# Spaced gathers, a ring of 28 blocks, a table for the drain, and one product, difference and sum for a tile's query rotations

## The reference, cut to what matters

```python
c_kv = x @ W_dkv                                   # 32 latents per key
I = index scores of 4 heads, local window = +inf, future = -inf
_, idx = top_k(I, 96)                              # 64 local keys and 32 chosen ones per query
key_c, value = (c_kv @ W_uk)[idx], (c_kv @ W_uv)[idx]
query_r = _pope((c_q @ W_qr), angles_q)            # softplus, then a rotation by the position
key_r = _pope((x @ W_kr)[idx], angles_k)           # angle by the rank in the list
scores = (query_c . key_c + query_r . key_r) * scale
out = softmax(scores) @ value                      # 8 heads, then @ W_out
# x1 = LN(x + out); a router picks 1 of 32 experts (capacity 80); x2 = LN(x1 + expert(x1))
# layer 2: 9 shifted gates and values, LN, 8 small experts and a shared one, LN
```

## Time and profile before

| what | value |
|---|---|
| three runs | 1228.55, 1239.28, 1255.21 us, median 1239.28 |
| the profiled execution | 1243.05 us |
| its span | 1240.8 us |
| mean granted TensorE clock | 0.817 of full |
| PE, DVE, ACT, POOL busy | 73%, 56%, 41%, 35% |
| chain that ended last | PE 50%, "another core or an unknown queue" 19%, issue 9%, ACT 9%, DVE 8% |

### The profile page before, as it was taken

One profiled execution on the slowest core, in us unless ns is written; L12 is line 12 of the kernel. 1 busy time (PEld: TensorE's weight loads), 2 busy tenths in 40 slices (PEclk: granted clock), 3 DMA queues, 4 the chain that ended last, 5 costly groups with the idle time before them and its releaser, 6 DMA issues.

```text
span 1240.8 us, 17636 instructions
## 1 busy us (share of the span) xinstructions
PE 909.5 (73%) x5786; PEld 518.2 (42%) x5786; DVE 689.6 (56%) x2059; ACT 509.4 (41%) x1463; POOL 431.8 (35%) x462
## 2 busy tenths in 40 slices
PE   7569639379379878787884965935529998878885
PEld 3235415236136544444442533623316584334443
DVE  4588608248248856573763762936303223887763
ACT  5256405134126646554543551814217322424420
POOL 3400360721710366665636054072640004320120
PEclk9588858679669988886977785966759989988987
DMA  8100211101100011111101010010106151000000
GB/s 227 29 1 22 36 27 26 39 20 33 30 17 4 16 27 22 26 23 22 26 12 26 6 21 19 5 25 14 22 20 175 34 148 44 6 1 10 1 9 17
DMA packets 59641, 39.97 MB, mean 32 GB/s; under 512 B 27072, under 2 KB 51360, under 8 KB 59424
## 3 DMA queue, kind: packets, MB, share of 16 engines
q1 hardware_dynamic: 44064, 23.40, 7.6%
q0 software_dynamic: 12800, 14.15, 5.6%
q10 hardware_dynamic: 2688, 1.31, 0.4%
HBM read 33.31 MB, written 5.55 MB: 31 GB/s over the span
## 4 chain that ended last, share of the span: by engine, by line
PE 50%; another core or an unknown queue 19%; issue 9%; ACT 9%; DVE 8%; DMA 2%; POOL 1%; SPq 0%; ACTq 0%; POOLq 0%; DVEq 0%
PE psK L726 6%; PE psI L636 5%; PE psK L622 4%; PE psP L788 3%; PE psS L762 3%; PE psP L795 3%; PE psS L1731 3%; ACT R L886 2%; PE psP L622 2%; PE psK L714 2%; PE psP L777 2%; PE psS L765 2%; ACT ot_region L1023 1%; PE psS L805 1%
## 5 line engine op out<-in xcount | busy, mean ns | idle before, releaser
L602 POOL DMA_INDIRECT G<-key_rows,idx x320 | 308.9, 965 | 483.3 <-DVEq L1126 238.3
L1014 ACT ACTIVATE PT<-psP 128x256 f32<-128x256 f32 x128 | 49.0, 383 | 408.8 <-remote 292.9
L1295 DVE CUSTOM_DVE_ANT_0 S<-psS,cst 128x208 f32<-128x208 f32 x128 | 47.5, 371 | 270.8 <-remote 207.7
L636 PE MATMUL psI<-kiT,qiT 64*128 64x512 f32 (+5 forms) x320 | 105.4, 675 | 64.9 <-ACT R L886 54.6
L622 PE MATMUL psK<-cst 128*128 128x512 bf16 x335 | 101.1, 416 | 14.5 <-issue 9.3
L762 PE MATMUL psS<-KT,Q 96*32 96x128 f32 x1024 | 70.7, 306 | 43.1 <-issue 26.7
L1099 DVE SCALAR_TENSOR_TENSOR SC<-R,w_i,SC 128x512 f32<-128x512 f32 (+5 forms) x120 | 78.5, 654 | 15.7 <-ACT R L886 12.8
L622 PE MATMUL psP<-cst 128*128 128x512 bf16 x114 | 46.0, 429 | 53.8 <-ACT ot_region L1023 46.9
L886 ACT ACTIVATE R<-psI 128x512 f32<-128x512 f32 (+5 forms) x160 | 73.6, 511 | 15.7 <-remote 6.5
L1129 DVE MAX8 top<-SC 128x8 f32<-128x128 f32 (+15 forms) x64 | 78.5, 1226 | 2.3
L1131 DVE FIND_INDEX8 idxf<-top,SC 128x8 uint32<-128x128 f32 (+15 forms) x64 | 78.3, 1223 | 0.0
(11 more groups left out here) (341 smaller groups left out, 1803.0 us busy)
## 6 DMA issues: line engine op xcount, KB each, us to landing
G<-key_rows,idx POOLq DMA_INDIRECT x320
rtmp<-idx_rows SPq DMA_DIRECT2D x32, 128.0 KB
xslots<-zrow SPq DMA_DIRECT2D x4, 320.0 KB, 9.0
SC<-xslots SPq DMA_DIRECT2D x8, 160.0 KB
yslots<-SC ACTq DMA_DIRECT2D x8, 160.0 KB, 2.9
V<-val_rows SPq DMA_DIRECT2D x15, 80.0 KB
xr<-in_x SPq DMA_DIRECT2D x1, 1024.0 KB, 9.4
qiT<-in_w_gate SPq DMA_DIRECT2D x4, 256.0 KB, 4.2
```

What stands on the lines that cost most here:

```text
L602: pool.indirect_dma_start(ring[o % RING][:, g % GPB, DR:], None, key_rows, bass.IndirectOffsetOnAxis(ap=idx[:, t, g:g + 1], axis=0),).then ...
L636: pe.matmul(psI[i][:, 0:w], lhs, kiT[64 * i:64 * i + 64, CH * c:CH * c + w], start=True, stop=True).then_inc(s["i_mm"], 1)
```

## The change

Five things. (1) **Gathers**: the wait of the second gather for the landing of the block before is gone. Ahead of the second, third and fourth gather of a block GpSimd sets 64 columns of a spare tile to zero and waits for its own increment. (2) **Ring**: four more slots lie in the memory of four weights that are dead after the start, so it has 28 blocks. (3) **Drain**: the stages of each tile have their steps in a table, one step earlier for the last two tiles (two for some), `WARM_T` is 0 and the filler matmuls of the drain have a table too; `place` is cut in two. (4) **Queries**: a tile's four products are one instruction, its differences one and its sums one. (5) **Second part**: the loads of slots go out ahead of those of weights, and a batch's first gather no longer waits for the landing of the batch before. Some semaphores are used twice.

```diff
-RING_G, RING_X = 21, 3
-RING = RING_G + RING_X
+RING_G, RING_X, RING_W = 21, 3, 4
+RING = RING_G + RING_X + RING_W
+SPACE = 64
-WARM_TILE, WARM_K, WARM_P, WARM_T = 10, 2, 1, 4
+WARM_TILE, WARM_K, WARM_P, WARM_T = 10, 2, 1, 0
+STAGES = {"add": (1, 0, 1), "norm_scale": (2, 0, 1), "normalize": (3, 0, 1), "x1_t": (5, 1, 2), "x1_copy": (6, 1, 2),
+          "router": (7, 1, 2), "route": (8, 1, 2), "gate_exp": (9, 1, 2), "cumulate": (9, 1, 2), "count": (10, 1, 2),
+          "place": (10, 0, 2)}
+WARM_TAIL = {1: 3, 2: 3, 3: 3, 4: 3, 5: 3, 6: 3, 8: 2, 9: 2, 10: 1, 12: 1, 14: 2, 15: 1}
+def stage_step(stage, t):
+    step, last_but_one, last = STAGES[stage]
+    return NB * (t + 2) + step - (last if t == NT - 1 else last_but_one if t == NT - 2 else 0)
...
+                            if g % GPB == 0 and o == RING - RING_W:
+                                pool.wait_ge(s["w_cp"], 3)
                             if g % GPB == 0 and o >= RING:
                                 pool.wait_ge(s["pv"], ring_block[o - RING] + 1)
-                            if g % GPB == 1 and o > FIXED:
-                                pool.wait_ge(s_g[(o - 1) % RING], gathered(o - 1))
+                            if g % GPB:
+                                link(pool.memset(spacer[:, :], 0.0))
                             pool.indirect_dma_start(
...
-                    if n > NT * NB:
-                        keep_warm(psK, 2 if n < NT * NB + NB else 3)
+                    keep_warm(psK, WARM_TAIL.get(n - NT * NB, 0))
-                    if n == NB * (NT + 1):
+                    if n == NB * (NT + 1) - 1:
                         out_project(NT - 1)
...
+                    mu = qmu[:, :, :, :].rearrange("p h k f -> p (h k) f")[:, None, :, :]
+                    dve.tensor_tensor(qt[:, :, :, :], mu.to_broadcast([P, 4, NH * 2, HALF]),
+                                      rot[:, 0:4, t, None, :].to_broadcast([P, 4, NH * 2, HALF]),
+                                      ALU.mult).then_inc(s["q_chain"], 1)
...
+                    dve.tensor_tensor(to[:, :, :, 0:HALF], tc[:, :, :, 0, :], ts[:, :, :, 1, :],
+                                      ALU.subtract).then_inc(s["q_chain"], 1)
+                    dve.tensor_tensor(to[:, :, :, HALF:DR], ts[:, :, :, 0, :], tc[:, :, :, 1, :],
+                                      ALU.add).then_inc(s["q_chain"], 1)
...
-        for g in range(NXB, NEG):
+        for g in range(NXB, NEG - 1):
             load_slots(g)
-            if g < NEG - 1:
-                sp.wait_ge(s["y_mm"], g - NXB + 1)
-                k["load_experts"](sp, g + 1)
+        for g in range(NEW, NEG):
+            sp.wait_ge(s["y_mm"], g - NEW + 1)
+            k["load_experts"](sp, g)
+            if g == NEW:
+                load_slots(NEG - 1)
...
-            if c >= 1:
-                pool.wait_ge(s_yg[c - 1], at_yg[c - 1] + 16 * TPC)
-            for t in batch(c):
+            for i, t in enumerate(batch(c)):
+                if i == 1 and c >= 1:
+                    pool.wait_ge(s_yg[c - 1], at_yg[c - 1] + 16 * TPC)
```

More of the change, by code:

```diff
@@ L125 @@
 N0, N1 = -2 * NB, NT * NB + 2 * NB + 3
+STAGES = {"add": (1, 0, 1), "norm_scale": (2, 0, 1), "normalize": (3, 0, 1), "x1_t": (5, 1, 2), "x1_copy": (6, 1, 2),
[5 more added lines that the diff above has]
+    return NB * (t + 2) + step - (last if t == NT - 1 else last_but_one if t == NT - 2 else 0)
+TILE_AT = {stage: {stage_step(stage, t): t for t in range(NT)} for stage in STAGES}
 INDEX_END = NB * (NT - 2) - -1
@@ L305, in program @@
         ring += [xT[:, GW * i:GW * (i + 1)].rearrange("p (j n) -> p j n", j=GPB) for i in range(RING_X)]
+        ring += [w_first[:, GW * i:GW * (i + 1)].rearrange("p (j n) -> p j n", j=GPB) for i in range(RING_W)]
         at = 2 * NG * P - NT * (DR + CKV) - NT * P
@@ L439, in program @@
         again += [(s_g[i], 64 * len(range(i + RING, len(ring_block), RING))) for i in range(FIXED)]
+        again += [(s["ld_raw"], 16), (s["ld_tab"], 16)]
         flat = G[:, :]
@@ L1077, in _ @@
                             q_evac(st + 1, 1)
[L1078 to L1084, removed]
+                    if n in TILE_AT["norm_scale"]:
+                        norm_scale(TILE_AT["norm_scale"][n])
+                    if n in TILE_AT["x1_copy"]:
+                        x1_copy(TILE_AT["x1_copy"][n])
+                    if n in TILE_AT["gate_exp"]:
+                        gate_exp(TILE_AT["gate_exp"][n])
                 second_scalar(act)
@@ L1200, in q_min @@
                     if t >= 1:
-                        dve.wait_ge(s["q_chain"], 10 * t)
+                        dve.wait_ge(s["q_chain"], 5 * t)
                     dve.tensor_scalar(qe[:, :, :, :], psM[:, NH * CKV:].rearrange("p (h k f) -> p h k f", h=NH, k=2),
                                       30.0, None, ALU.min).then_inc(s["q_chain"], 1)
[L1205 to L1222, removed]
@@ L1338, in route, with count @@
                                       ALU.is_equal).then_inc(s["rt"], 1)
-                def place(t):
+                def count(t):
                     dve.wait_ge(s["cum_mm"], t + 1)
@@ L1346, in place @@
                                              accum_out=rsm[:, 3:4]).then_inc(s["rte"], 1)
+                def place(t):
                     dve.wait_ge(s["rte"], t + 1)
@@ L1396, in _ @@
                             topk_step(t, i)
-                    if 0 <= st - 2 < NT and b == 1:
-                        row_stats(st - 2)
-                    if 0 <= st - 3 < NT and b == 2:
-                        place(st - 3)
+                    if n in TILE_AT["add"]:
+                        row_stats(TILE_AT["add"][n])
+                    if n in TILE_AT["count"]:
+                        count(TILE_AT["count"][n])
+                    if n in TILE_AT["place"]:
+                        place(TILE_AT["place"][n])
                 second_vector(dve)
@@ L1457, in second_part @@
     s_yg, at_yg = zip(*k["again"][NXB + 2:NXB + 2 + NCH])
-    s_out = [sem(f"t_out{i}") for i in range(2)]
+    s_out, at_out = zip(*k["again"][NXB + 2 + NCH:NXB + 4 + NCH])
     stt3 = m["mvs"][:, 0:6 * TPC].rearrange("p (t n) -> p t n", t=TPC)
@@ L1520, in second_gpsimd @@
                                         ).then_inc(s_yg[c], 16)
-        done = [0]
+        done = [3]
         def root(n_stats, dst=rstd[:, :], src=mv[:, :, 1]):
@@ L1912, in second_vector @@
         lnn = [8 * (NCH - 1)]
-        pooln = [0]
+        pooln = [3]
         def statistics(src, after):
```

85 lines of the change are left out of this document (46 added, 39 removed).

## The result

| | before | after | ratio, 95% interval |
|---|---|---|---|
| median us | 1240.85 (4 runs, 1228.55 to 1255.21) | 1199.80 (4 runs, 1196.84 to 1203.22) | 0.970, 0.962 to 0.978 |
| profiled execution, its span | 1243.05, 1240.8 | 1201.29, 1199.2 | |
| granted TensorE clock | 0.817 | 0.811 | |

What follows compares the result with a forecast made beforehand. TensorE's reports held back by gathers were taken as the bound. From the profiled 1243: -142 + 6 - 3 - 2 - 3 - 3 = 1096, and some +4, gave 1100 us; range of 8 in 10: 1035 to 1250.

Steps and rivals of the forecast that it cites:

- the debt: Gathers: each holds back TensorE's reports about 1.42 us, 5.68 per block of four, growing 0.48 per block in bursts.
- The 221 us: Seven stretches of 21 to 35 gathers in a row, 318 us: 734 matmuls that would need 97 us at 7.54 per us.
- 55 out of the paced stretch: Stretch where the ring is full and gathers wait for `pv`: 1267 matmuls in 223 us, 55 us lost.
- Part (1), the memset's price: Gaps between a block's gathers: 0.50 us in place of 0.31, so a block takes 5.60 us (5.0 to 6.4).
- rival B: Gap between gathers too small (0.41 us, block 5.33), or the cause is not pace: 1233 or 1232 us; chance 0.29 together.
- Part (1), what it buys: Bursts of gathers: 5.68 matmuls per us throughout, 1072 more matmuls, -142 us, and +6 for longer bursts.
- The first ten microseconds of a burst: Start of a run of gathers: 53 matmuls, about the paced 5.68 per us, taken as the rate for whole bursts.
- Part (2), the ring: Ring of 28: 15 blocks of tiles 8 to 12 go unpaced; taken as 0, +33 us if bursts cost as now.
- rival C: Ring turns paced blocks into bursts, spacing worth nothing: 1265 us, 1278 with part (4) and a cold drain; chance 0.13.
- Parts (3) and (5), the drain and the second part: Drain: -3 for fillers, -2 for earlier stages. Second part: -3 for slots, -3 for the batches' first gathers.
- Part (4): Queries' products in one instruction: some 0.3 us of VectorE less in 16 tiles, not the bound: 0, or +8 if it shows.
- The +4 us: Allowance for what the queries' joined product and the drain's fillers may cost, raising the sum from 1096 to 1100 us.

Runs made afterwards that it cites:

- the hold: Kind of comparison in which the kernel before took 1224 to 1241 us (four comparisons); in the other kind it took 933 to 935 (three).
- run 670: Not a run of a kernel: 670 is the number of matmuls that the six bursts would have run in 290 us at 2.31 per us.
- the second comparison: Changed kernel unedited and with memsets of 256 columns in place of 64, beside the kernel before: 1162.57 (0.950) and 999.47 us (0.816) against 1223.63.

## Why the prediction was right in its sign and wrong in its size

**The bound and the debt: right.** 1.41 to 1.44 us per gather came out at paces of 5.0, 5.2 and 5.4 us per block, from 32, 33 and 35, with all bytes and half of them. Take the hold away and ScalarE's unexplained wait is gone; without it the kernel before is 290 us faster. The 221 us that I read out of the bursts and 55 out of the paced stretch are of that size. Small slips in the working change nothing: the four gathers of the paced stretch give (6.08 - 0.25) / 4 = 1.46, not 1.42 to 1.45, and the rows hold 219 issues in the bursts, at most 55 blocks, where I wrote 57.

**Part (1), the memset's price: right on the average, and that hid something.** Forecast 5.60 us per block, measured 5.40 in tiles 5 to 7 and 5.69 in tiles 13 to 15. In the early bursts the gap is 0.44 us, nearly rival B's 0.41, and the debt grows by 0.28 per block. I had one pace for all bursts.

**Part (1), what it buys: wrong, and the step that failed.** The prediction put it as "If whole bursts run at that rate, their 318 us hold 1806 matmuls", the rate being 5.68 matmuls per us: -142 +6 us. The bursts ran at 2.55 in tiles 5 to 7 and 3.91 in tiles 13 to 15. In the early ones the premise fell, since the block stayed 0.28 us below the debt. In the late ones the gap was as forecast and the debt small (2.6 us at the last burst's end), and the rate stayed below 5.68 all the same: I read the debt as something that hurts when large, and it hurts at zero growth too. That the reports wait for a moment without any debt is my reading of this; shown is that relief came with 0.3 to 0.6 us more per block. Priced by matmuls: the six bursts ran 941 in 290 us, 3.24 per us; at the 2.31 of before they would have run 670; the 271 more are 36 us at 7.54 per us, and with the 9 us of tile 0 it is 45, where I had 136 for the part. The first ten microseconds of a burst were no model for the rest, then or now (85 matmuls in ten, then 64 in 26). ScalarE's unexplained wait, which was to fall below 100 us, fell to 270.3.

**Part (2), the ring: 0 is neither refuted nor shown.** Without spacing the kernel took 1276, inside rival C's 1265 to 1278, though there only as an experiment, and C's mechanism shows: tile 11's blocks take 5.0 us in place of 6.1 and run 2.99 matmuls per us in place of 5.70. But this kernel also lacks the old wait for the landing, so the 1276 are not the ring's alone. With the spacing the 18 us mix ring and pace, as said above. In the first result tiles 8 to 12 run at 4.8 per us in place of 5.68 and get longer pauses.

**Parts (3) and (5), the drain and the second part.** Forecast -11 together. From the start of tile 15 to the last scatter it is 51.3 us before (940.7 to 992.0) and 42.9 after (906.9 to 949.9): -8.4, where I had -5. No filler stands ahead of the last six transpositions now, and the clock did not fall (1.00 in that stretch, 0.92 from tile 15 to the end, before and after). The experts take 2.5 us less, as forecast for the slots. The batches' first gather gave nothing with the hold, and the chain of waits shows why:

```profile
985.95 1.00 POOL R L1540
...
989.77 2.50 DMA R<-yslots,slot_out
...
995.09 5.09 another core or an unknown queue
1001.39 7.46 another core or an unknown queue
1008.87 0.61 ACT G L1824
```

The old waits had let the debt of the second part's gathers run off (4.11 us from a batch to its landing). Now 16 go out in 19.7 us, and TensorE's first products for the second layer are heard only at 1008.87. From the first of these gathers to the end the changed kernel's forms need 209.5 to 213.3 us with the hold and 206 to 208.6 in seven profiles without; the old form needed 210 with it (one profile) and 209 and 212 without. So the 3 us seem to be there without the hold, and with it they are paid back or more; with so few profiles of the old form this is not firm.

**Part (4): more than I had, and it doesn't matter.** Groups by form:

```profile
L1229 DVE TENSOR_TENSOR qt<-qmu,rot 128x1024 f32<-128x1024 f32 x16 | 19.7, 1228 | 0.6
L1243 DVE TENSOR_TENSOR QF<-qt 128x256 f32<-128x256 f32 x16 | 6.7, 417 | 0.0
L1241 DVE TENSOR_TENSOR QF<-qt 128x256 f32<-128x256 f32 x16 | 6.5, 408 | 0.0
```

The products fall from 24.2 us to 19.7. I had 0.3 us per tile for "four starts less", which are three; the rows say 0.28. The joined differences and sums come on top: 13.2 us where the rows before have 9.3 and 9.1, another 0.33 per tile. What this is worth in the kernel's time was not measured alone. The +4 us that I put in for part (4) and the fillers show in no run.

**The page's rule.** The rows show TensorE's progress changing from 7.88 matmuls per us to 2.14 (94 in 44 us of a burst without memsets) by the pace of gathers alone. The Trainium skill ("SBUF — State Buffer", Who interferes with whom) says that a DMA never contends with a compute engine. Where the hold is absent the trace agrees (8.3 per us in the loop, gathers at full pace in it). Where it is present the rule would have told me to expect nothing of the spacing, and 1276 us without memsets against 999 with 256 columns speaks against that.

## What to carry to other kernels

When work is held up by a rate, find the rate first, then stay clear of it: 5.68 us of debt in blocks of 5.40 to 5.69 us gave 61 us in the second comparison, and half a microsecond more per block gave 224, 3.7 times as much. Check the pace in every stretch: one block of 5.68 us read at the end of the trace hid bursts of 5.40 at its start, and an edit of the ring moved it by 0.3 us. Measure such a change at two or three gaps, since the price of a gap (here 0.5 us more per block for 192 columns more) is known long before its worth. And run the kernel before beside every comparison: its own time moved by 290 us from one comparison to another with nothing changed, and the best version differed. With the hold it is 256 columns (999 us, better than before and after by 18% and 14%); without it, none (900 us, 3.8% better than before).

## What the runs showed of the hardware that I had not expected

- **The hold comes and goes.** Beside gathers back to back ScalarE's copy stood idle up to 34.4 us without a known releaser with the hold, and at most 4.5 without it, then released by TensorE: one kernel, two comparisons. One chip showed both kinds. Within a comparison all runs agreed. What differs between them isn't in the trace.
- **1.42 us per gather or scatter of 128 indices**, at 64 or 32 numbers per index, at blocks of 5.0, 5.2 and 5.4 us (1.44 in the last).
- **A start behind a linked memset takes 0.27 or 0.56 us**, by the place of the instruction in the list and not by the length of the memset: 0.56 stood behind memsets of 64, 256 and 512 columns (0.17, 0.33 and 0.54 us). In every kernel with memsets between its gathers and a ring of 28 it stood behind 0 of 72 memsets in tiles 5 to 7 and 27 of 72 in tiles 13 to 15; in the three kernels with such memsets and a ring of 24 behind 3 of the latter. I don't know the reason; it makes a block 0.3 us longer.
